# Entry of a cross-attention layer: row statistics split over VectorE and GpSimd, keys and values ahead of the turned rows, context loads between weight loads

## The reference, cut to what matters

```python
x = x + _L0_xattn_ref(_layernorm(x, axis=-1), ctx_1024, ctx_1024, ...)   # changed at its entry
x = x + _L0_ffn_ref(_layernorm(x, axis=-1), ...)
x = x + _L1_xattn_ref(_layernorm(x, axis=-1), ctx_1024, ...)
x = x + _L1_ffn_ref(_layernorm(x, axis=-1), ...)

def _L0_xattn_ref(q, k, v, w_q, b_q, w_k, b_k, w_v, b_v, w_o, b_o):      # D_MODEL 128, H 16, D_K 8
    query = q @ w_q.T + b_q          # q: the normalised rows of x
    key_, value = k @ w_k.T + b_k, v @ w_v.T + b_v                       # k, v: the context
    scores = einsum('bhqd,bhkd->bhqk', query, key_) / sqrt(8)
    x = einsum('bhqk,bhkd->bhqd', softmax(scores), value)
    return x @ w_o.T + b_o
```

## Time and profile before

| what | us |
|---|---|
| median of 3 runs | 716.19 |
| the runs | 719.8, 715.73, 716.19 |
| the profiled execution, its own time | 715.08 |
| its span in the profile | 713.3 |

### The profile page before, as it was taken

How to read it: one execution, slowest core, us unless ns; L and a number is a source line. 1 busy time by engine, 2 the same in 40 slices (tenths; PEclk the granted TensorE clock), 3 DMA queues, 4 the chain that set the end, 5 groups by cost and what they waited for, 6 DMA issues and landing times.

```text
span 713.3 us, 16734 instructions
## 1 busy us (share of the span) xinstructions
PE 666.7 (93%) x6575; PEld 568.9 (80%) x6582; DVE 449.7 (63%) x1177; ACT 337.3 (47%) x914; POOL 121.2 (17%) x221
## 2 busy tenths in 40 slices
PE   6699989999999999989999999899999999998985
PEld 2478779898888889877777777699999999954774
DVE  5489858747855755779999999543334344453443
ACT  1589862324222222337888888445555454410320
POOL 2225850022000000004300000000000000004575
PEclk8899999999999999999999999899999999988998
DMA  7600200000000000023422200000000001041110
GB/s 245 201 17 17 66 3 1 1 1 1 1 1 1 0 1 1 1 57 98 99 68 70 68 7 5 2 1 1 1 17 17 16 1 28 12 96 41 52 59 29
DMA packets 30088, 25.03 MB, mean 35 GB/s; under 512 B 3887, under 2 KB 26801, under 8 KB 29762
## 3 DMA queue, kind: packets, MB, share of 16 engines
q1 hardware_dynamic: 28418, 20.91, 10.4%
q0 software_dynamic: 1600, 3.15, 1.5%
HBM read 19.33 MB, written 5.51 MB: 35 GB/s over the span
## 4 chain that ended last, share of the span: by engine, by line
PE 40%; DVE 8%; issue 4%; DMA 1%; POOL 1%; ACT 0%; POOLq 0%; DVEq 0%
PE SC L890 5%; PE MI L630 3%; PE PT L620 3%; PE SC L808 3%; PE SC L850 2%; PE SC L855 2%; PE SC L814 2%; PE SC L811 2%; PE PT L861 2%; PE SC L611 2%; DVE mx L1298 2%; DVE sc L1295 2%; PE SC L980 2%; DVE kexp L1278 2%; PE MI L989 1%
## 5 line engine op out<-in xcount | busy, mean ns | idle before, releaser
L1112 ACT ACTIVATE big<-SC 128x512 f32<-128x512 f32 x88 | 52.6, 600 | 144.5 <-PE SC L703 144.4
L713 PEld LDWEIGHTS PT<-wd,big 128*128 128x128 f32 (+1 forms) x768 | 90.2, 191 | 2.8 <-issue 0.4
L713 PE MATMUL PT<-wd,big 128*128 128x128 f32 (+1 forms) x768 | 90.7, 274 | 0.0
L1439 DVE TENSOR_TENSOR big<-SC,big 128x512 f32<-128x512 f32 (+1 forms) x88 | 60.5, 689 | 41.7 <-PE SC L703 32.4
L703 PE MATMUL SC<-xP,wgP 128*128 128x512 f32 x264 | 78.8, 407 | 0.7 <-DVE big L1439 0.3
L703 PE MATMUL SC<-xP,wuP 128*128 128x512 f32 x264 | 74.6, 391 | 0.0
L630 PEld LDWEIGHTS MI<-vblk,PTs 128*64 128x64 f32 x1536 | 49.8, 139 | 11.2 <-ACT oT L1059 2.9
L703 PEld LDWEIGHTS SC<-xP,wuP 128*128 128x128 f32 x264 | 49.6, 188 | 10.9
L630 PE MATMUL MI<-vblk,PTs 128*64 128x18 f32 x1536 | 54.2, 213 | 3.9 <-ACT big L1064 1.7
L1054 ACT ACTIVATE PTs<-PT 128x512 f32<-128x512 f32 x96 | 52.2, 594 | 7.5 <-PE PT L620 6.5
L620 PE MATMUL PT<-ident,sc 128*128 128x128 f32 x384 | 54.0, 285 | 0.6 <-ACT sc L1049 0.6
(11 more groups left out here) (255 smaller groups left out, 1321.1 us busy)
## 6 DMA issues: line engine op xcount, KB each, us to landing
kvs<-in_ctxT SPq DMA_DIRECT2D x32, 64.0 KB, 2.0
w1s<-in_e1w SPq DMA_DIRECT2D x8, 256.0 KB, 3.0
w2s<-in_e1w SPq DMA_DIRECT2D x8, 256.0 KB, 3.0
wg<-in_wg SPq DMA_DIRECT2D x1, 1408.0 KB, 9.0
wu<-in_wu SPq DMA_DIRECT2D x1, 1408.0 KB, 12.0
wd<-in_wd SPq DMA_DIRECT2D x2, 512.0 KB, 14.1
x_mid<-X SPq DMA_DIRECT2D x1, 1024.0 KB, 5.1
X<-x_mid SPq DMA_DIRECT2D x4, 256.0 KB, 4.7
```

Source lines behind the costliest of these rows:

```text
L713: last = pe.matmul(PT[:, e % 2, t * P:t * P + P], h[0:w, t * P:t * P + P], wd[0:w, e, c, :], start=(c == 0), stop=(c == 2))
L1112: act.activation(sg[a % 2], SC[:, a % 2, :], ACT.Silu).then_inc(s["silu_done"], 1)
L1439: last = dve.tensor_tensor(hT[e % 2][0:w, c, :], SC[0:w, 2 + a % 2, :], sg[a % 2][0:w, :], ALU.mult)
```

## The change

1. **VectorE** takes statistics of tiles 0 to 3 only, their roots and group 0's rows; then the statistics of tiles 4 to 7; and those of 8 to 11 and 12 to 15 around its first two `front`s.
2. **GpSimd** makes the roots of tiles 4 to 7, the rows of group 1, the roots of tiles 8 to 15, and the rows of groups 2 and 3. Only then it adds the bias to X and waits for the expert weights.
3. **TensorE** makes K and V of tile 0 before any row is turned (K in bank PT, which VectorE's `front` then reads without waiting for Q or V copies), turns group 0, makes K of tile 1, then both Qs and V of tile 1. The turnings of groups 1, 2 and 3 stand before step 0, in step 0 and in step 1. The folds come after the third projection.
4. **ScalarE** follows that order; `rows_kept` of groups 2 and 3 stand behind `exp` of steps 0 and 1.
5. **SyncE**: contexts 2, 3, 4 and 5 are issued between `lw`, `f1`, `wg`, `wu` and `wd`, each behind its own wait for `proj_done`.
6. The second block of matmuls on zeros starts after 6 steps of the root chain, not 8, and has 7 matmuls, not 8; the pairs between the turnings are gone.

```diff
@@ SyncE
             load0(0, 0)
+            load0(1, 1)
             sp.dma_start(lw[:, :, :], io["lw"]).then_inc(s["lstm_w_loaded"], 16)
-            load0(1, 1)
+            load0(2, 0)
             sp.dma_start(f1[:, :], io["f1"]).then_inc(s["lstm_w_loaded"], 16)
+            load0(3, 1)
             sp.dma_start(wg[:, :, :], io["wg"]).then_inc(s["moe0_w_loaded"], 16)
+            load0(4, 0)
             sp.dma_start(wu[:, :, :], io["wu"]).then_inc(s["moe0_w_loaded"], 16)
+            load0(5, 1)
...
-            for n in range(2, NU0):
+            for n in range(6, NU0):
                 load0(n, n % 2)
@@ GpSimd
+            def rsqrt_of(a, b):
+                pool.wait_ge(s["ln_stats"], b)
+                mean_of(a, b)
+                variance_of(a, b)
+                for _ in range(3):
+                    refine_of(a, b)
+            rsqrt_of(4, 8)
+            rows_of(xn[1], 4, 0, 4)
+            rsqrt_of(8, NT)
+            for m in (2, 3):
+                pool.wait_ge(s["ln_transposed"], m - 1)
+                rows_of(xn[m % 2], 4 * m, 0, 4)
             pool.wait_ge(s["ln_xn"], GRP)
             pool.tensor_tensor(X[:, :, :], X[:, :, :], rows[:, 0:1, :].broadcast_to([P, NT, D]), ALU.add
@@ TensorE
-            pe.wait_ge(s["ln_newton"], 8)
-            keep_warm(SC[:, 0, :], 8)
+            pe.wait_ge(s["ln_newton"], 6)
+            keep_warm(SC[:, 0, :], 7)
...
-            for q in range(GRP):
-                wait(pe, s["ln_evacuated"], q - 1)
-                rows_turned(q, TPB[q % 2])
-                if q:
-                    keep_warm(SC[:, 1, :], 2)
+            pe.wait_ge(s["prep_done"], 1)
             pe.wait_ge(s["attn_w_loaded"], 16 * N_ATTN)
-            pe.wait_ge(s["prep_done"], 1)
-            pe.wait_ge(s["ln_evacuated"], GRP)
...
+                if known(n, 0, 1):
+                    rows_turned(n + 2, MI)
                 if not known(n, NU0 - 3, NU0 - 2, NU0 - 1):
                     proj(0, n + 3, n + 3, 1 - p)
+                if known(n, 1):
+                    pe.wait_ge(s["ln_evacuated"], GRP)
...
+            pe.wait_ge(kv_loaded[0], 16)
+            pe.matmul(PT[:, 0, 0:P], wat[:, 2, :], kvs[0][:, :], start=True, stop=True)
+            pe.matmul(PJ[:, 2 * P:3 * P], kvs[0][:, :], wat[:, 3, :], start=True, stop=True
+                      ).then_inc(s["proj_done"], 1)
+            rows_turned(0, MI)
+            pe.wait_ge(kv_loaded[1], 16)
+            pe.matmul(PT[:, 1, 0:P], wat[:, 2, :], kvs[1][:, :], start=True, stop=True).then_inc(s["second_k"], 1)
+            pe.wait_ge(s["v_copied"], 1)
+            pe.wait_ge(s["ln_evacuated"], 1)
+            for n in range(2):
+                pe.matmul(PJ[:, n * P:n * P + P], wat[:, 1, :], xnT[:, n * P:n * P + P], start=True, stop=True)
+            pe.matmul(PJ[:, 2 * P:3 * P], kvs[1][:, :], wat[:, 3, :], start=True, stop=True
+                      ).then_inc(s["proj_done"], 1)
             scores(0, 0, "soft_done", 0)
...
+            pe.wait_ge(s["q_ready"], 2)
+            pe.wait_ge(s["v_copied"], 2)
             proj(0, 2, 2, 0)
+            first_fold(0)
+            first_fold(1)
+            rows_turned(1, MI)
             pe.wait_ge(s["fold_copied"], 2)
@@ ScalarE, step0
+                if known(n, 0):
+                    for u in range(2):
+                        fold_copy(u)
+                    rows_kept(1, MI)
...
                 exp(n, p)
+                if known(n, 0, 1):
+                    rows_kept(n + 2, MI)
@@ VectorE
-            stats(0, NT)
-            dve.wait_ge(s["ln_stats"], NT)
-            rsqrt(0, NT)
-            for q in range(GRP):
-                normalise(q)
+            stats(0, 4)
+            dve.wait_ge(s["ln_stats"], 4)
+            rsqrt(0, 4)
+            normalise(0)
+            stats(4, 8)
             dve.wait_ge(s["prep_done"], 1)
             front(0, 0, 0)
+            stats(8, 12)
             front(0, 1, 1)
+            stats(12, NT)
```

More of the change, by code:

```diff
@@ L384, in _ @@
             pool.sem_inc(s["prep_done"], 1)
[L386 to L398, removed]
             tiny = [0]
@@ L435, in rows_of, with resid @@
                     last.then_inc(s["ln_xn"], 1)
+            def rsqrt_of(a, b):
[10 more added lines that the diff above has]
+                rows_of(xn[m % 2], 4 * m, 0, 4)
+            pool.wait_ge(s["ln_xn"], GRP)
+            pool.tensor_tensor(X[:, :, :], X[:, :, :], rows[:, 0:1, :].broadcast_to([P, NT, D]), ALU.add
+                               ).then_inc(s["bo_added"], 1)
+            pool.wait_ge(s["bo_added"], 1)
+            pool.wait_ge(s["moe0_w_loaded"], 16 * N_MOE)
+            def resid(n, p):
+                pool.wait_ge(s["xo_ready"], n + 1)
+                xt = X[:, bass.ds(n, 1), :].rearrange("p a d -> p (a d)")
+                pool.tensor_tensor(xt, xo[p][:, :], xt, ALU.add).then_inc(s["resid_done"], 1)
             def first_rows(n):
@@ L566, in rows_turned @@
                 pe.wait_ge(s["ln_xn"], m + 1)
+                if m < GRP:
+                    wait(pe, s["ln_evacuated"], m)
                 for t in range(4):
@@ L636, in out_t, with first_fold @@
                 pe.transpose(MI[:, 0:P], on[p][:, :, :], ident[:, :]).then_inc(s["ot_done"], 1)
-            for q in range(GRP):
-                wait(pe, s["ln_evacuated"], q - 1)
-                rows_turned(q, TPB[q % 2])
-                if q:
-                    keep_warm(SC[:, 1, :], 2)
-            pe.wait_ge(s["attn_w_loaded"], 16 * N_ATTN)
-            pe.wait_ge(s["prep_done"], 1)
-            pe.wait_ge(s["ln_evacuated"], GRP)
+            pe.wait_ge(s["prep_done"], 1)
+            pe.wait_ge(s["attn_w_loaded"], 16 * N_ATTN)
+            def first_fold(u):
+                pe.wait_ge(s["kexp_ready"], u + 1)
+                pe.wait_ge(s["lstm_w_loaded"], 16 * N_LSTM)
+                pe.matmul(PT[:, u, :], wat[:, 4 + 4 * u, :], lw[:, 1, :], start=True, stop=True
+                          ).then_inc(s["fold_done"], 1)
             def out0(n, p):
@@ L1033, in q_copy @@
             def q_copy(a, n, p):
-                act.wait_ge(s["proj_done"], n + 1)
-                act.activation(qT[p][:, :], PJ[:, 0:P], ACT.Identity, bias=cols[:, C_BQ[a]:C_BQ[a] + 1],
+                first = known(n, 0, 1)
+                act.wait_ge(s["proj_done"], 2 if first else n + 1)
+                act.activation(qT[p][:, :], PJ[:, n * P:n * P + P] if first else PJ[:, 0:P], ACT.Identity, bias=cols[:, C_BQ[a]:C_BQ[a] + 1],
                                scale=QSCALE).then_inc(s["q_ready"], 1)
@@ L1088, in step0, with fold_copy @@
                 exp(n, p)
+                if known(n, 0, 1):
+                    rows_kept(n + 2, MI)
                 if n == NU0 - 1:
                     rows_kept(GRP, PJ)
[L1091 to L1097, removed]
+            v_copy(0, 0)
+            rows_kept(0, MI)
+            q_copy(0, 0, 0)
+            q_copy(0, 1, 1)
+            v_copy(1, 1)
+            def fold_copy(u):
+                act.wait_ge(s["fold_done"], u + 1)
+                act.activation(lwo[u][:, 0:P], PT[:, u, 0:P], ACT.Copy, scale=0.5)
+                act.activation(lwo[u][:, P:2 * P], PT[:, u, P:2 * P], ACT.Copy)
+                act.activation(lwo[u][:, 2 * P:4 * P], PT[:, u, 2 * P:4 * P], ACT.Copy, scale=0.5
                                ).then_inc(s["fold_copied"], 1)
@@ L1271, in front @@
             def front(a, n, p):
-                dve.wait_ge(s["q_ready"], n + 1)
-                dve.wait_ge(s["v_copied"], n + 1)
+                if known(n, 0, 1):
+                    dve.wait_ge(s["second_k" if n else "proj_done"], 1)
+                    k_bank = PT[:, n, 0:P]
+                else:
+                    dve.wait_ge(s["q_ready"], n + 1)
+                    dve.wait_ge(s["v_copied"], n + 1)
+                    k_bank = PJ[:, P:2 * P]
                 wait(dve, s["scores_done"], n - 1)
-                k_in = PJ[:, P:2 * P].unsqueeze(1).broadcast_to([P, HR, P])
+                k_in = k_bank.unsqueeze(1).broadcast_to([P, HR, P])
                 alone = hm[:, :].unsqueeze(2).broadcast_to([P, HR, P])
```

11 lines of the change are left out of this document (3 added, 8 removed).

## The result

The changed kernel has a median of 720.03 us over nine runs (718.6 to 725.53); the kernel before, in nine runs beside it, 716.79 (715.73 to 720.71). The ratio is 1.0062, 95% interval 1.0035 to 1.0089: slower by 0.6%, less than the 1% that the chances go by, and 2.4 us above the predicted 717.6. Of these 2.4 us 0.6 is the kernel before, whose median was 716.19 over the three runs that the forecast started from and is 716.79 over nine; the change itself cost 3.2 us, not 1.4. The profiled execution took 720.0 us with a span of 718.1 (before 715.08 and 713.3), +4.8 in the span.

The account below looks back on a forecast made before the run. The prediction took GpSimd's root chains and rows to bound the entry. `pv` of tile 0 at 39.6 against 38.22 gave +1.4, added to the 716.19 median: 717.6 us, middle forecast chance 0.50, range 713.0 to 721.5.

Parts of the forecast that it names:

- the class (within 1%): Whole kernel: a time within 1% (7.2 us) of the kernel before, chance 0.93; slower 0.04, faster 0.03.
- The entry: First 40 us, until the attention's steady period: `pv` of tile 0 at 39.6 instead of 38.22, +1.4 us.
- VectorE and GpSimd: Entry: GpSimd starts at 14.05, needs 0.284 us a link, and ends rows of groups 1 to 3 at 23.2, 32.4, 35.6.
- TensorE ahead of step 0: Entry: TensorE ready for turning group 2 at 28.6, then waits about 4 us; early keys, ordering and context loads stay hidden.
- Steps 0 and 1: Entry, from the turning of group 2 at 32.5: lower clock at first, `pv` of tile 0 at 39.6, +1.4 us.
- so I take 38.2 again: Entry, steps 0 and 1: the full clock returns at about 38.2, as in the kernel before.
- The cost of the lower clock: Steps 0 and 1: `pv` at 39.6; rival with full clock from 32.5: 38.3, total 716.3, chance 0.17.
- Loads: SyncE's queue: `wd` landed at 44.1, before the first `xo_copy` at 47.1 needs it; no effect on time.
- The late weights: Rival: `wd` lands at 50.9, first `xo_copy` and projection 6 stand 3.8 us; 722.4, chance 0.10.
- Blocked GpSimd: Rival: large VectorE operations block GpSimd's chain in the entry, rows 4 to 6 us later; 722 to 724, chance 0.06.
- The early-rows rival: Turning of group 2: rows come earlier, 714.5; never late, 713.8; with full clock too, 712.5; chance 0.17.
- Everything behind the attention shifted by one constant: After the entry: same 3.95 us period, and all later work shifted by the same amount as `pv` of tile 0.

Follow-up runs that it names:

- the three pairs: Kernel before and changed kernel, both unedited, profiled three times each, one pair per group; the first pair is the profiled execution of the result.
- `pool_plus8`: Changed kernel with two more refinement steps (8 small GpSimd instructions) in the root chain of tiles 8 to 15: 722.31 us, ratio 1.0083 to the kernel before.
- The second profile: Changed kernel, no edit, profiled and timed again: 719.22 us, ratio 1.0057 to the kernel before.
- the third: Changed kernel, no edit, profiled a third time in another group: one execution, 727.68 us, beside 727.49 for the kernel before.
- `warm_gap`: Changed kernel with 9 and 28 matmuls on zeros in TensorE's two waits for GpSimd's rows: 718.97 us, ratio 1.0027 to the kernel before.
- `old_loads`: Changed kernel with the old load order, contexts 2 to 15 behind all of `wd`: 722.63 us, ratio 1.009 to the kernel before.
- `before_loads`: Kernel before with context 2 ahead of `wg`, 3 ahead of `wu`, 4 and 5 ahead of `wd`: 714.81 us, ratio 0.9977 to the kernel before.
- `pad_dve`: Changed kernel with 12 small VectorE instructions added in step 0, refining roots no longer used: 724.16 us, ratio 1.0012 to the kernel before.
- `split_rows`: Changed kernel with roots of tiles 8 to 15 and rows of groups 2 and 3 on VectorE: 710.4 us, later 716.23; ratios 0.9899, 0.9881 to the kernel before.

## Why the prediction was right or wrong

The sign, the range and the class (within 1%) were right. The size was not: +3.2 us for a forecast of +1.4. That the total is as near as it is owes something to luck. The entry, where the whole +1.4 was to lie, gave +0.54, +0.98 and -0.40 in the three pairs, and most of the measured difference lies behind it, where I had priced nothing.

- **VectorE and GpSimd.** GpSimd starts at 14.03 (forecast 14.05). Group 1 ends at 23.2, group 2 is turned from 32.54, group 3 ends at 35.60 (forecast 23.2, 32.4, 35.6). One link of this chain in other work carried over exactly, and so did the claim that the rows bound the entry; `pool_plus8` shows it directly.
- **TensorE ahead of step 0.** Forecast ready by 28.6, in fact 25.4. I had doubled 5.6 us of work, waits and all, for the lower clock. In the first profile that work ran at 1.00. In the second it ran at the lower level from 15.4 to 22.3 and still took only 7.4 us (15.88 to 23.25) for a price of 11.2; there TensorE was ready at 24.8. The wait became 7.1 and 7.7 us, not 4, without consequence for the time, since the rows decide.
- **Steps 0 and 1.** The failed step is "so I take 38.2 again" for the clock's return: it was back at 37.0 in the first profile and 36 in the second, before the turning of group 3. In the third it was back at 38.1, as assumed, and `pv` came at 39.10; the half microsecond that is left there lies in the prices of the steps. In the first profile that turning took 0.66, not the lower-clock 0.95, and projection 4 ended at 38.7, not 39.4. `pv` came at 38.76 and 38.70 for a forecast of 39.6. I had carried over when it came back in one execution of the kernel before; the three profiles of that kernel alone have its `pv` between 37.72 and 39.50, so one execution was too little to go by.
- **The cost of the lower clock.** I had put it at 39.6 - 38.3 = 1.3 us; `warm_gap` took 1.1 to 1.2 back. The Trainium skill, TensorE: Matmul & The Clock Gate, "HAM oscillation — how this bites in real kernels", says that waits between bursts of matmuls bring the lower rate. The second profile agrees: the clock fell at 29, inside the wait of 7.7 us, and was back at 36. In the first it had fallen at 23.4, after the wait of 2.4 us for group 1's rows and ahead of the long one. The fall at 340.5 followed no such wait.
- **Loads.** Forecast landed at 44.1; the last piece, issued at 36.44, took 6.5 and landed at 42.9. Nothing waits near 46, and the first output copy is at 46.26 (forecast 47.1). The late weights fell away. "Worth nothing in time" for the context loads was right for the changed kernel as a whole, but `old_loads` shows that the cover was thinner than I said: with the old order of loads `pv` is 2.85 us later.
- **Blocked GpSimd.** It fell away too. The subtraction, with its large input in PSUM and `mx` in SBUF, ran beside the chain without blocking it. The Trainium skill, SBUF — State Buffer, "Who interferes with whom", says that a VectorE instruction with at most one SBUF input, outside certain modes, does not contend with GpSimd; the trace agrees, as the links beside this subtraction kept their 0.28 us. The timeline of the changed kernel, around 27 us:

```profile
26.75 0.20 POOL L417 TENSOR_TENSOR rstd<-nw,rstd 128x8 f32<-128x8 f32 x1
26.78 1.22 DVE L1342 TENSOR_TENSOR sc<-SC,mx 128x1024 f32<-128x1024 f32 x1
27.03 0.20 POOL L414 TENSOR_TENSOR nw<-rstd 128x8 f32<-128x8 f32 x1
27.31 0.20 POOL L415 TENSOR_TENSOR nw<-nw,var 128x8 f32<-128x8 f32 x1
27.60 0.20 POOL L416 TENSOR_SCALAR nw<-nw 128x8 f32<-128x8 f32 x1
27.88 0.20 POOL L417 TENSOR_TENSOR rstd<-nw,rstd 128x8 f32<-128x8 f32 x1
```

- **The early-rows rival** had the right mechanism and the wrong floor. I let TensorE arrive at the turning at 28.6 and got 713.8, or 712.5 at full clock. With the rows in time it turns group 2 at 24.66 and `pv` comes at 30.42 to 30.50, at least 7.2 us earlier than in any profile of the kernel before, with 1% less time. The floor came from the doubled prices and from serial turnings; I had bounded the term that mattered least for the forecast and most for what the change could be.
- **"Everything behind the attention shifted by one constant"** failed. Of the 3.2 and 3.6 us between the medians of the two comparisons, the entry holds 0.5 to 1.0. The stalls in VectorE's stream hold about 1.6. Between the same VectorE instructions, at full clock (times of the kernel before), the changed program is longer by 0.50 from 145 to 195 us, by 0.08 from 254 to 316, by 0.56 from 389 to 454 (0.36 and twice 0.11 of it the stalls at the product) and by 0.48 from 531 to 584, in the LSTM; other stalls are taken up again by a later wait. In the same stretches the five profiles with 1177 VectorE instructions (three of the kernel before, `before_loads`, `pad_dve`) agree with each other within 0.05. `pad_dve` is not distinguishable from the kernel before in time; but the changed kernel itself was not timed in several rounds on that chip, so no run measures their share of the time. A fall of the clock near 400 us, some 1.2 us, came in three of the six profiles with this VectorE program and in none of the eight others. Whether the stalls bring it, where about one further us lies, and what decides the falls at 322 and 340, stays open.

## What to carry to other kernels

When work is moved to a slower engine, add up its chain to the moment when each piece is needed, before pricing anything that the reordering saves: here 21 + 21 small links of 0.28 us and the rows of eight tiles, 0.8 each, hid a gain of 7 us in the entry, and handing only the second half of them back to VectorE brought 1%. Then price the rival "this engine is in time" as carefully as the forecast, for that is the version to build. For effects under 1% look at several profiles of both kernels; a single one showed a fall of the clock worth 4 us that did not come back in the two others. And when an effect is small, look at stretches that the change doesn't touch: a different number of instructions ahead moved stalls there.

## What the runs showed of the hardware

- VectorE stalls at fixed places of its program, and they move with the number of instructions ahead. It lost 0.36 us between a reciprocal and its product near 394 us, and 0.11 at the same product in two further passes of the loop, in six profiles of six with the same VectorE program; twelve more instructions at 22 to 25 us took all of it away. Each of the stalls of about 0.35 us goes with an 8 KB packet of kind "instruction" on the DMA queue q14, which starts 0.66 to 0.96 us after the delayed instruction.
- The granted clock of one program differs between executions at the same place: 0.52 or 1.00 in 340.5 to 350.5 us, with TensorE busy 10.00 and 9.92 of 10 us, and the fall came after 3.44 busy us of 3.50 at full clock.
- In one and the same kernel (`split_rows`) executions with an average granted clock from 0.973 to 0.987 took from 713.1 down to 704.8 us.
